# A windowed-attention kernel: the values projected together with queries and keys, in one group of 384 columns, and split at once into eight buffers

## The chip, the core and the metric

The kernel runs on one core of a Trainium2 chip (trn2). The core has TensorE (PE, with its weight loads PEld), VectorE (DVE), ScalarE (ACT), GpSimd (POOL) and SyncE (SP), each with its own stream of instructions; they wait for one another by semaphores. SBUF holds the data, PSUM (eight banks of 512 FP32 columns on each of 128 partitions) the results of TensorE. The metric is the device time of one execution in microseconds (us), lower is better.

## The reference, cut to what matters

A block of a Swin transformer (layer norm, attention in shifted windows of 8 x 8 with rotary embedding, a gated MLP), followed by self-attention over each image. The change touches only the first attention. x is (4, 32, 32, 128); there are 64 windows of 64 tokens, 16 heads of 8 channels.

```python
xs = jnp.roll(xn, (-SS[0], -SS[1]), axis=(1, 2))
xw = xs.reshape(B, nH, wh, nW, ww, DIM).transpose(0, 1, 3, 2, 4, 5).reshape(B_, N, DIM)
qkv = xw @ qkv_w.T + qkv_b
qkv = qkv.reshape(B_, N, 3, HEADS, HD).transpose(2, 0, 3, 1, 4)
q, k, v = (qkv[0], qkv[1], qkv[2])
q = _rope2d(q.reshape(-1, wh, ww, HD), tabs).reshape(B_, HEADS, N, HD)
k = _rope2d(k.reshape(-1, wh, ww, HD), tabs).reshape(B_, HEADS, N, HD)
attn = jnp.einsum('bhnd,bhmd->bhnm', q * scale, k)
attn = attn.reshape(B, nWin, HEADS, N, N) + attn_mask[None, :, None]
attn = jax.nn.softmax(attn.reshape(B_, HEADS, N, N), axis=-1)
out = jnp.einsum('bhnm,bhmd->bhnd', attn, v).transpose(0, 2, 1, 3).reshape(B_, N, DIM)
```

## The kernel before, in words

Two windows (128 tokens) make a pair; there are 32 pairs. The layer norm works in 8 chunks of 4 pairs. Precision is kept by splitting FP32 values into two FP16 parts, a high and a low one, so a product is three matmuls (high by high, high by low, low by high), and a projection has a fourth for the bias.

The attention stage is a software pipeline over steps n = -2 to 34, written as one `body(n, ...)` per engine; each engine does its own body in written order, so the order in the code is the order of the work. Steps -2 to 11 and 28 to 34 are unrolled, 12 to 27 are two rounds of a loop of eight steps. In step n:

- TensorE projects the queries and keys of pair n+2 (lines 866 and 868, `project`, into bank 4, 256 columns), turns the rows of pair n+1 (line 904), adds the mask and the scores of pair n (lines 876 and 885), in some steps turns a chunk of the layer norm (line 845), makes the turned scores of pair n-1 (876 and 897), multiplies probabilities by values for pair n-3 (line 956, 24 matmuls), projects the values of pair n-1 (866 and 868 again, 128 columns, into bank 6), and turns the queries of pair n with their maxima (line 904).
- VectorE multiplies queries and keys of pair n+2 by the two rope tables (line 1048, ta and tb), copies the turned rows of pair n+1 (line 1060, qk_t), makes the low part of the values of pair n-2 (line 1068, v_lo), takes the row maxima of pair n (line 1075), writes them in two parts into q_rows (lines 1080 and 1082), and normalises the result of pair n-3 (lines 1093 and 1097).
- ScalarE copies the rotated rows of pair n+2 (line 1117, q_rows and k_rows), takes the exponential for pair n-1 (line 1187), copies the turned queries (q_t), copies the high part of the values of pair n-1 (v_hi), and that of the probabilities (p_hi). `copy` is a helper, so all copies have line 1117; the tile tells them apart. In steps 3 to 10 it also normalises half a chunk (line 1131, xn) at the end of the step.
- GpSimd adds ta and tb into rot (line 1253), makes the low part of the probabilities of pair n-2 (line 1261, p_lo), and the low parts of the rows of pair n+2 (lines 1265 and 1267).
- SyncE copies keys from qk_t to k_t, four transfers a step (line 836).

The semaphores around the change: `qk_done` (projection of queries and keys done), `rope_done` (tb done, so bank 4 is free), `v_done` (values projected), `vhi_done`, `vlo_done` (their parts made), `mlo_done` (line 1082 done; the turning of the queries waits for it), `mask_hi` (mask copied to BF16). v_hi and v_lo have two buffers each. Each v buffer keeps zeros where the other window of the pair is, and a constant column; GpSimd writes both at the start (line 1222).

The mask copy of ScalarE stands in step -1, behind two transfers that it issues; TensorE waits for it ahead of step 0. The first steps of the MLP (`early`) are woven into steps 28 to 34.

## Time and profile before

| | us |
|---|---|
| median of 3 runs | 410.07 |
| lowest, highest | 408.0, 411.35 |
| profiled execution, its own time | 408.14 |
| its span in the trace | 406.3 |
| attention stage, first rope to last | about 12 to 190 |

| engine | busy us of the span |
|---|---|
| PE | 357.3 (88%) |
| DVE | 300.9 (74%) |
| ACT | 272.5 (67%) |
| POOL | 261.0 (64%) |

Busy time is the time in which at least one instruction of the engine ran. In a timeline each row has the start and the duration; "x3" merges three instructions of one kind that follow each other, and an instruction may start before the one ahead of it has written its last element. What stands in brackets is idle time of the engine before the row and what ended it.

### The profile page before, as it was taken

How to read it: one execution, taken by the hardware profiler on the slowest of the kernel's cores; microseconds unless marked ns; L12 is line 12 of the kernel's file. 1: busy time of each engine (PE TensorE's matmuls, PEld its weight loads, DVE VectorE, ACT ScalarE, POOL GpSimd, SP SyncE). 2: the span in 40 equal slices, each digit the busy share in tenths (PEclk: the TensorE clock that was granted, in tenths of full speed). 3: DMA queues.
4: the chain of work that ended last, by engine and by line, in shares of the span. 5: the costliest groups of instructions: out<-in, count | busy, mean ns of one | idle time of the engine just before them, and what ended most of it. 6: DMA issues, size and time to landing. Idle time of an engine off the chain costs nothing.

```text
span 406.3 us, 12124 instructions
## 1 busy us (share of the span) xinstructions
PE 357.3 (88%) x4700; PEld 223.4 (55%) x4700; DVE 300.9 (74%) x830; ACT 272.5 (67%) x436; POOL 261.0 (64%) x314
## 2 busy tenths in 40 slices
PE   2487999899998999998599999999989989989692
PEld 0244665555565666667355345553546757667472
DVE  6668888888888888887746767778657797884524
ACT  3467988887777787887635554444767867768480
POOL 7467967666767777797658665564235865868330
PEclk9999999999999999999989999999999999999787
DMA  5701110001101011110000100000101011010101
GB/s 173 250 15 27 29 27 26 25 24 30 31 27 29 25 29 29 29 29 3 0 3 2 26 2 0 2 2 0 28 0 28 2 52 27 2 54 2 53 2 55
DMA packets 15594, 12.19 MB, mean 30 GB/s; under 512 B 3991, under 2 KB 14136, under 8 KB 15544
## 3 DMA queue, kind: packets, MB, share of 16 engines
q1 hardware_dynamic: 14208, 10.96, 9.4%
q8 instruction: 34, 0.56, 0.6%
q10 hardware_dynamic: 1336, 0.54, 0.5%
q14 instruction: 16, 0.13, 0.1%
HBM read 4.15 MB, written 2.10 MB: 15 GB/s over the span
## 4 chain that ended last, share of the span: by engine, by line
PE 63%; DVE 15%; ACT 5%; DMA 5%; issue 5%; POOL 3%; SPq 2%; ACTq 1%; DVEq 0%; POOLq 0%
PE ps L347 8%; PE ps L1551 7%; PE ps L876 6%; PE ps L904 5%; PE ps L956 4%; PE ps L897 4%; DMA k_t<-qk_t 3%; PE ps L866 3%; PE ps L885 3%; PE ps L361 3%; SPq L836 2%; PE ps L868 2%; DVE ob L1687 2%; PE ps L1386 2%; DVE mx L1656 2%
## 5 line engine op out<-in xcount | busy, mean ns | idle before, releaser
L1738 POOL TENSOR_TENSOR el<-e,eh 128x1024 f16<-128x1024 f32 x28 | 59.7, 2131 | 42.0 <-ACT eh L1730 41.7
L1261 POOL TENSOR_TENSOR p_lo<-e_buf,p_hi 128x1024 f16<-128x1024 f32 x32 | 68.2, 2131 | 4.9 <-ACT p_hi L1117 2.9
L347 PE MATMUL ps<-y_t,fc_w 128*128 128x512 f16 x192 | 46.4, 383 | 4.0 <-POOL al L273 2.5
L1253 POOL TENSOR_TENSOR rot<-ta,tb 128x256 f32<-128x256 f32 x32 | 23.3, 728 | 38.9 <-DVE tb L1048 38.1
L1723 ACT ACTIVATE e<-ps 128x1024 f32<-128x1024 f32 x32 | 32.7, 1022 | 21.1 <-PE ps L1540 19.5
L1551 PE MATMUL ps<-val,eh 128*128 128x129 f16 x512 | 38.3, 225 | 7.5 <-DVE ob L1687 7.0
L876 PE MATMUL ps<-mask,identb 128*128 128x512 bf16 x128 | 39.4, 391 | 5.4 <-DMA k_t<-qk_t 5.2
L1075 DVE TENSOR_REDUCE ps<-ps 128x16 f32<-128x1024 f32 x32 | 39.4, 1233 | 6.0 <-PE ps L885 5.2
L1187 ACT ACTIVATE e_buf<-ps 128x1024 f32<-128x1024 f32 x32 | 32.7, 1023 | 14.5 <-PE ps L897 11.4
L1551 PEld LDWEIGHTS ps<-val,eh 128*128 128x128 f16 x512 | 32.8, 100 | 16.4 <-issue 9.9
L288 POOL TENSOR_TENSOR hl<-hid,hh 128x512 f16<-128x512 f32 x24 | 27.6, 1157 | 21.5 <-DVE yn L537 11.5
L1656 DVE TENSOR_REDUCE mx<-ps 128x1 f32<-128x1024 f32 x24 | 29.3, 1222 | 11.0 <-PE ps L1524 10.8
L1117 ACT ACTIVATE p_hi<-e_buf 128x1024 f16<-128x1024 f32 x32 | 33.8, 1057 | 0.8
L1730 ACT ACTIVATE eh<-e 128x1024 f16<-128x1024 f32 x32 | 33.7, 1054 | 0.7
L646 ACT ACTIVATE sg<-ps,fc_bias 128x512 f32<-128x512 f32 x32 | 21.9, 685 | 17.9 <-PE ps L347 17.6
L508 DVE SCALAR_TENSOR_TENSOR hid<-ps,fc_bias,sg 128x512 f32<-128x512 f32 x32 | 23.9, 746 | 11.2 <-PE ps L347 8.9
L866 PE MATMUL ps<-qkv_w,xn_all 128*128 128x128 f16 (+1 forms) x192 | 27.7, 255 | 5.0 <-ACT mask L1117 3.4
L904 PE MATMUL ps<-ident,q_rows 128*128 128x128 f16 x256 | 26.3, 227 | 6.0 <-DVE q_rows L1082 3.7
L347 PEld LDWEIGHTS ps<-y_t,fc_w 128*128 128x128 f16 x192 | 17.3, 98 | 25.9 <-issue 4.7
L1117 ACT ACTIVATE q_t<-ps 128x512 f16<-128x512 f16 x32 | 19.1, 596 | 10.7 <-PE ps L904 10.4
L897 PEld LDWEIGHTS ps<-q_t,k_t 128*64 128x64 f16 x1024 | 18.7, 113 | 13.6 <-issue 13.6
L1551 PE MATMUL ps<-val,el 128*128 128x129 f16 x256 | 23.8, 226 | 0.0
(166 smaller groups left out, 959.8 us busy)
## 6 DMA issues: line engine op xcount, KB each, us to landing
k_t<-qk_t SPq DMA_DIRECT2D x126, 32.0 KB, 1.9
x_all<-in_x SPq DMA_DIRECT2D x8, 256.0 KB, 4.9
out<-ob SPq DMA_DIRECT2D x8, 192.0 KB, 2.1
yr<-xr SPq DMA_DIRECT2D x16, 64.0 KB, 2.0
mask_f<-in_mask SPq DMA_DIRECT2D x1, 512.0 KB, 3.7
fc_w<-in_fc_w SPq DMA_DIRECT2D x1, 512.0 KB, 6.2
out<-ob SPq DMA_DIRECT2D x4, 128.0 KB, 2.4
fc_w<-in_fc_w SPq DMA_DIRECT2D x1, 256.0 KB, 6.1
```

What stands on the lines that cost most here:

```text
L347: last = pe.matmul(ps[:, bank, :], fc1_w16[:, ws, 128 * block_:128 * block_ + 128], y_t[:, v, ys, :], start=(n == 0), stop=(n == 2))
L866: pe.matmul(out, xn_all[:, at(i, 1), xs, :].rearrange("p a q -> p (a q)"), qkv_w16[:, ws, cols], start=(n == 0), stop=False, skip_group_ch ...
L876: pe.matmul(ps[:, bank + b, :].rearrange("p (h k) -> p h k", h=8), identb[:], mm, start=(part == 0), stop=False, skip_group_check=True)
L897: last = pe.matmul(ps[rows, ST_BANK + h // 8, WTOK * (h % 8):WTOK * (h % 8) + WTOK], keys[:, h % 4, h // 4, rows], queries[:, h // 4, rows ...
L904: last = pe.transpose(out[:, c, :], rows[:, 4 * c:4 * c + 4, :].rearrange("p h r -> p (h r)"), ident16[:])
L1075: dve.tensor_reduce(mx_ps, ps[:, S_BANK:S_BANK + 2, :].rearrange("p b (h k) -> p (b h) k", h=8), AX.X, ALU.max).then_inc(max_done, 1)
L1117: return act.activation(out, in_, ACT.Copy)
L1261: pool.tensor_tensor(p_lo[:, u], e_buf[:, u], p_hi[:, u], ALU.subtract).then_inc(plo_done, 1)
L1551: return pe.matmul(pv4[:, j, i, 0:DIM + 1], weights[:, T % H_BUFS, 128 * n:128 * n + 128], val[:, b % 2, part, m, 0:DIM + 1], start=first, ...
L1656: dve.tensor_reduce(mx[:, k:k + 1], two(S4), AX.X, ALU.max, negate=True).then_inc(max4_done, 1)
L1730: act.activation(eh[:, T % H_BUFS, :], e4[:, T % E_BUFS, :], ACT.Copy).then_inc(eh_done, 1)
L1738: pool.tensor_tensor(el[:, T % H_BUFS, :], e4[:, T % E_BUFS, :], eh[:, T % H_BUFS, :], ALU.subtract).then_inc(el_done, 1)
```

## The change

- The values are projected with queries and keys: each of the four matmuls of `project` has 384 columns instead of 256, into bank 4, for pair n+2. The group of four matmuls with 128 columns and its semaphore `v_done` are gone.
- v_hi and v_lo of pair n+2 are made in step n: v_hi at the front of ScalarE's step, behind `rope_done`; v_lo on VectorE at the place where v_lo of pair n-2 was, ahead of the maximum. The projection of the next pair waits for `vlo_done` too.
- v_hi and v_lo have eight buffers instead of two. GpSimd clears them as FP32 words (1152 on each partition for each, where it was 576 FP16 values).
- The mask is copied on ScalarE before step -2, and TensorE waits for it in step 0 ahead of the first scores, behind the projection of pair 2 and the turning of pair 1.
- The first turning of the MLP waits for `vlo_done` of all pairs instead of `rope_done`.

```diff
--- before.py
+++ after.py
@@ -118,8 +118,10 @@
         mask_f = until_mlp.enter_context(nc.sbuf_tensor("mask_f", [128, 2, WPAIRS, WTOK], F32))
         mask16 = until_mlp.enter_context(nc.sbuf_tensor("mask16", [128, 3, 2, WPAIRS, WTOK], BF16))
         xn_all = until_mlp.enter_context(nc.sbuf_tensor("xn_all", [128, PAIRS, 2, 128], F16))
-        v_hi = until_mlp.enter_context(nc.sbuf_tensor("v_hi", [128, 2, HP, 2, 2, HD + 1], F16))
-        v_lo = until_mlp.enter_context(nc.sbuf_tensor("v_lo", [128, 2, HP, 2, 2, HD + 1], F16))
+        v_hi_flat = until_mlp.enter_context(nc.sbuf_tensor("v_hi", [128, WPAIRS * HP * 4 * (HD + 1)], F16))
+        v_hi = v_hi_flat[:].rearrange("p (n h e r d) -> p n h e r d", n=WPAIRS, h=HP, e=2, r=2)
+        v_lo_flat = until_mlp.enter_context(nc.sbuf_tensor("v_lo", [128, WPAIRS * HP * 4 * (HD + 1)], F16))
+        v_lo = v_lo_flat[:].rearrange("p (n h e r d) -> p n h e r d", n=WPAIRS, h=HP, e=2, r=2)
 
         q_rows = until_mlp.enter_context(nc.sbuf_tensor("q_rows", [128, BUFS, HEADS, ROWS], F16))
         k_rows = until_mlp.enter_context(nc.sbuf_tensor("k_rows", [128, 2, HEADS, ROWS], F16))
@@ -172,7 +174,6 @@
         ln_ready = sem("ln_ready")
 
         qk_done = sem("qk_done")
-        v_done = sem("v_done")
         rope_done = sem("rope_done")
         vhi_done = sem("vhi_done")
         vlo_done = sem("vlo_done")
@@ -464,7 +465,7 @@
             def early(left):
                 if left == 5:
 
-                    pe.wait_ge(rope_done, PAIRS)
+                    pe.wait_ge(vlo_done, PAIRS)
                     turn_a_waits(0)
                     turn_a(0, 0)
                 if left == 4:
@@ -767,7 +768,7 @@
             S_BANK, ST_BANK, QKV_BANK, T1_BANK, T2_BANK, PV_BANK = 0, 2, 4, 5, 6, 7
             qkv_ps = ps[:, QKV_BANK, :]
             mx_ps = ps[:, S_BANK, 0:HEADS]
-            v_ps = ps[:, T2_BANK, 256:256 + DIM]
+            v_ps = ps[:, QKV_BANK, 2 * DIM:3 * DIM]
             t1_ps = ps[:, T1_BANK, :].bitcast(F16).rearrange("p (a c q) -> p a c q", a=2, c=4)
             t2_ps = ps[:, T2_BANK, 0:256].bitcast(F16).rearrange("p (c q) -> p c q", c=4)
             pv_ps = ps[:, PV_BANK, 0:HP * 4 * (HD + 1)].rearrange("p (h e r d) -> p h e r d", h=HP, e=2, r=2)
@@ -914,7 +915,8 @@
                         wait(pe, rope_done, n + 2)
 
                         pe.wait_ge(ln_ready, (n + 2) // TPC + 1 if isinstance(n, int) and n < LOOP_FROM else CHUNKS)
-                        project(qkv_ps[:, 0:2 * DIM], n + 2, slice(0, 2 * DIM)).then_inc(qk_done, 1)
+                        wait(pe, vlo_done, n + 2)
+                        project(qkv_ps[:, 0:3 * DIM], n + 2, slice(0, 3 * DIM)).then_inc(qk_done, 1)
                     if at_step(n, -2):
 
                         pe.wait_ge(mask_top, 1)
@@ -933,6 +935,8 @@
                         turn(t1_ps[:, 1], k_rows[:, v]).then_inc(t1_done, 1)
                     if valid(n, 0):
 
+                        if at_step(n, 0):
+                            pe.wait_ge(mask_lo if parts > 1 else mask_hi, 1)
                         pe.wait_ge(kz_ready[u], it * 64 + 64)
                         wait(pe, mlo_done, n)
                         scores(qk_t[:, u, 0], k_t[:, r], w, parts).then_inc(s_done, 1)
@@ -954,14 +958,9 @@
                             out = pv_ps[:, hp].rearrange("p e r d -> p (e r d)")
                             for k, (p, vals) in enumerate(((p_hi, v_hi), (p_hi, v_lo), (p_lo, v_hi))):
                                 last = pe.matmul(out, p[:, v, 2 * hp:2 * hp + 2, :].rearrange("p h q -> p (h q)"),
-                                                 vals[:, v, hp].rearrange("p e r d -> p (e r d)"),
+                                                 vals[:, (w - 3) % WPAIRS, hp].rearrange("p e r d -> p (e r d)"),
                                                  start=(k == 0 and hp == 0), stop=(k == 2), skip_group_check=True)
                         last.then_inc(pv_done, 1)
-                    if valid(n, 1):
-
-                        wait(pe, vlo_done, n - 1)
-                        wait(pe, q2_ready, n)
-                        project(v_ps, n - 1, slice(2 * DIM, 3 * DIM)).then_inc(v_done, 1)
                     if valid(n, 0):
                         wait(pe, mlo_done, n + 1)
                         wait(pe, q2_ready, n)
@@ -973,7 +972,6 @@
                 first_steps(lambda n, it, r: body(n, it, r, 1))
 
                 def other_pairs(parts):
-                    pe.wait_ge(mask_lo if parts > 1 else mask_hi, 1)
                     other_steps(pe, lambda n, it, r: body(n, it, r, parts), mlp_pe(pe)[1])
 
                 return rest[0], other_pairs
@@ -1060,14 +1058,15 @@
                         dve.tensor_copy(qk_t[:, v], t1_ps).then_inc(qt_ready, 1)
                     if at_step(n, -1):
                         ln_stats_of(3)
-                    if valid(n, 2):
-
-                        dve.wait_ge(vhi_done, n - 1)
+                    if valid(n, -2):
+
+                        dve.wait_ge(vhi_done, n + 3)
                         for e in range(2):
                             rows = slice(64 * e, 64 * e + 64)
                             last = dve.tensor_tensor(
-                                v_lo[rows, u, :, e, :, 0:HD], v_ps[rows, :].rearrange("p (h r d) -> p h r d", r=2, d=HD),
-                                v_hi[rows, u, :, e, :, 0:HD], ALU.subtract)
+                                v_lo[rows, (w + 2) % WPAIRS, :, e, :, 0:HD],
+                                v_ps[rows, :].rearrange("p (h r d) -> p h r d", r=2, d=HD),
+                                v_hi[rows, (w + 2) % WPAIRS, :, e, :, 0:HD], ALU.subtract)
                         last.then_inc(vlo_done, 1)
                     if valid(n, 0):
 
@@ -1145,6 +1144,8 @@
                 copy(qkv_w16[:, 0, :], w_scaled[:, 0:3 * DIM]).then_inc(qkv_w_hi, 1)
                 ln_hi_of(0)
                 ln_norm_of(1)
+                act.wait_ge(mask_loaded, 16)
+                copy(mask16[:, 0], mask_f[:]).then_inc(mask_hi, 1)
 
                 def body(n, it, w):
                     r = w % BUFS
@@ -1154,6 +1155,13 @@
                         mlp_act(act)[2](LAST - n)
                     if valid(n, -2):
 
+                        act.wait_ge(rope_done, n + 3)
+                        wait(act, pv_done, n - 5)
+                        for e in range(2):
+                            rows = slice(64 * e, 64 * e + 64)
+                            last = copy(v_hi[rows, (w + 2) % WPAIRS, :, e, :, 0:HD],
+                                        v_ps[rows, :].rearrange("p (h r d) -> p h r d", r=2, d=HD))
+                        last.then_inc(vhi_done, 1)
                         act.wait_ge(r_done, n + 3)
                         copy(q_rows[:, (r + 2) % BUFS, :, 0:16].rearrange("p h (r d) -> p h r d", r=2),
                              rot[:, u, 0].unsqueeze(2).broadcast_to([128, HEADS, 2, HD]))
@@ -1168,8 +1176,6 @@
                         for j in (2, 3):
                             rows = slice(ROWS * j, ROWS * j + ROWS)
                             act.dma_start(k_t[rows, 0, j], qk_t[rows, 0, 1]).then_inc(kz_ready[0], 16)
-                        act.wait_ge(mask_loaded, 16)
-                        copy(mask16[:, 0], mask_f[:]).then_inc(mask_hi, 1)
                         ln_norm_of(2)
                     if at_step(n, 0):
                         ln_norm_of(3)
@@ -1192,13 +1198,7 @@
                         copy(q_t2[:, u], t2_ps).then_inc(q2_ready, 1)
                     if valid(n, 1):
 
-                        act.wait_ge(v_done, n)
                         wait(act, pv_done, n - 2)
-                        for e in range(2):
-                            rows = slice(64 * e, 64 * e + 64)
-                            last = copy(v_hi[rows, v, :, e, :, 0:HD],
-                                        v_ps[rows, :].rearrange("p (h r d) -> p h r d", r=2, d=HD))
-                        last.then_inc(vhi_done, 1)
                         act.wait_ge(exp_done, n)
                         copy(p_hi[:, v], e_buf[:, v]).then_inc(phi_done, 1)
                     if at_step(n, 0):
@@ -1214,7 +1214,7 @@
             def _(pool):
 
 
-                for k, (part, value) in enumerate(((v_hi[:], 0.0), (v_lo[:], 0.0),
+                for k, (part, value) in enumerate(((v_hi_flat[:].bitcast(F32), 0.0), (v_lo_flat[:].bitcast(F32), 0.0),
                                                    (v_hi[0:64, :, :, 0, :, HD:HD + 1], WSCALE),
                                                    (v_hi[64:128, :, :, 1, :, HD:HD + 1], WSCALE))):
                     if k >= 1:
```

How it stands on ScalarE, in a step between 5 and 10 that ends with half a normalisation. q_rows and k_rows are the rotated rows, e_buf the exponential, q_t the turned queries, xn the normalised chunk. Before, from the exponential on:

```order
L1187 ACTIVATE e_buf<-ps 128x1024
L1117 ACTIVATE q_t<-ps 128x512
L1117 ACTIVATE v_hi<-ps 64x8x2x8 x2
L1117 ACTIVATE p_hi<-e_buf 128x1024
L1131 ACTIVATE xn<-x_all,nmr,rstd 128x128 x2
L1117 ACTIVATE q_rows<-rot 128x16x16
L1117 ACTIVATE k_rows<-rot 128x32x8
```

And of the change (its line numbers differ by a few):

```order
L1193 ACTIVATE e_buf<-ps 128x1024
L1116 ACTIVATE q_t<-ps 128x512
L1116 ACTIVATE p_hi<-e_buf 128x1024
L1130 ACTIVATE xn<-x_all,nmr,rstd 128x128 x2
L1116 ACTIVATE v_hi<-ps 64x8x2x8 x2
L1116 ACTIVATE q_rows<-rot 128x16x16
L1116 ACTIVATE k_rows<-rot 128x32x8
```

v_hi stood between q_t and p_hi; it now stands behind p_hi and xn, ahead of the next q_rows.

On TensorE, where one step goes over to the next, from the last product with the values on. Before:

```order
L956 MATMUL ps<-v_hi,p_lo 128x36
L866 MATMUL ps<-qkv_w,xn_all 128x128 x3
L868 MATMUL ps<-qkv_b,sel 128x128
L904 MATMUL ps<-ident,q_rows 128x128 x4
L866 MATMUL ps<-qkv_w,xn_all 128x256 x3
L868 MATMUL ps<-qkv_b,sel 128x256
L904 MATMUL ps<-ident,q_rows 128x128 x4
L904 MATMUL ps<-ident,k_rows 128x128 x4
```

And now:

```order
L960 MATMUL ps<-v_hi,p_lo 128x36
L905 MATMUL ps<-ident,q_rows 128x128 x4
L867 MATMUL ps<-qkv_w,xn_all 128x384 x3
L869 MATMUL ps<-qkv_b,sel 128x384
L905 MATMUL ps<-ident,q_rows 128x128 x4
L905 MATMUL ps<-ident,k_rows 128x128 x4
```

The four matmuls of 128 columns ahead of the turning of q_rows are gone, and the projection behind it has 384 columns. VectorE's instructions keep their order; only the pair that v_lo works on is another.

## Rows read from the trace of the kernel before

**Rows 1.** Windows view: busy us of PE, PEld, DVE, ACT, POOL; clock, DMA, GB/s
```profile
140.00:150.00 10.00, 10.00 (x185) 6.39 (x184) 8.94 (x24) 8.23 (x15) 7.88 (x11) 1.00 0.10 26
```

**Rows 2.** Timeline, VectorE, one step: start us, duration us, instruction, [idle before]
```profile
147.32 0.23 DVE L1082 SCALAR_TENSOR_TENSOR q_rows<-ps,q_rows 128x16 f16<-128x16 f32 x1
...
148.66 0.42 DVE L1048 TENSOR_TENSOR ta<-ps,rope 128x256 f32<-128x256 f32 x1 [0.26 <-PE ps L868]
149.00 0.42 DVE L1048 TENSOR_TENSOR tb<-ps,rope 128x256 f32<-128x256 f32 x1
149.33 0.68 DVE L1060 COPY qk_t<-ps 128x1024 f16<-128x1024 f16 x1
149.93 0.59 DVE L1068 TENSOR_TENSOR v_lo<-ps,v_hi 64x128 f16<-64x128 f32 x2
150.54 1.23 DVE L1075 TENSOR_REDUCE ps<-ps 128x16 f32<-128x1024 f32 x1
...
152.07 0.23 DVE L1082 SCALAR_TENSOR_TENSOR q_rows<-ps,q_rows 128x16 f16<-128x16 f32 x1
```

**Rows 3.** Timeline, TensorE, the same step
```profile
147.15 0.33 PE L866 MATMUL ps<-qkv_w,xn_all 128*128 128x128 f16 x3
147.41 0.23 PE L868 MATMUL ps<-qkv_b,sel 33*128 33x128 f16 x1
147.60 0.40 PE L904 MATMUL ps<-ident,q_rows 128*128 128x128 f16 x4
147.91 0.50 PE L866 MATMUL ps<-qkv_w,xn_all 128*128 128x256 f16 x3
148.34 0.28 PE L868 MATMUL ps<-qkv_b,sel 33*128 33x256 f16 x1
```

**Rows 4.** Timeline, ScalarE, the same step
```profile
148.04 0.60 ACT L1117 ACTIVATE q_t<-ps 128x512 f16<-128x512 f16 x1 [0.37 <-PE ps L904]
148.53 0.59 ACT L1117 ACTIVATE v_hi<-ps 64x128 f16<-64x128 f32 x2
149.14 1.06 ACT L1117 ACTIVATE p_hi<-e_buf 128x1024 f16<-128x1024 f32 x1
```

**Rows 5.** Timeline, ScalarE, a step with half a normalisation
```profile
60.68 1.06 ACT L1117 ACTIVATE p_hi<-e_buf 128x1024 f16<-128x1024 f32 x1
61.64 0.86 ACT L1131 ACTIVATE xn<-x_all,nmr,rstd 128x128 f32<-128x128 f32 x2
62.41 0.40 ACT L1117 ACTIVATE q_rows<-rot 128x256 f16<-128x256 f32 x1
```

**Rows 6.** Timeline, VectorE, line 1082 in steps 3, 11 and 29
```profile
42.81 0.23 DVE L1082 SCALAR_TENSOR_TENSOR q_rows<-ps,q_rows 128x16 f16<-128x16 f32 x1
...
85.57 0.23 DVE L1082 SCALAR_TENSOR_TENSOR q_rows<-ps,q_rows 128x16 f16<-128x16 f32 x1
...
175.85 0.23 DVE L1082 SCALAR_TENSOR_TENSOR q_rows<-ps,q_rows 128x16 f16<-128x16 f32 x1
```

**Rows 7.** Timelines of VectorE and TensorE at the start
```profile
12.42 0.42 DVE L1048 TENSOR_TENSOR ta<-ps,rope 128x256 f32<-128x256 f32 x1 [0.68 <-PE ps L868]
...
13.27 0.85 PE L866 MATMUL ps<-qkv_w,xn_all 128*128 128x256 f16 x3
...
14.48 0.42 DVE L1048 TENSOR_TENSOR ta<-ps,rope 128x256 f32<-128x256 f32 x1 [1.25 <-PE ps L868]
...
18.59 0.38 DVE L996 BATCH_NORM_AGGREGATE mv<-stats 128x2 f32<-128x6 f32 x4
...
20.22 0.82 PE L866 MATMUL ps<-qkv_w,xn_all 128*128 128x256 f16 x3 [3.38 <-ACT mask L1117]
```

**Rows 8.** Timelines of VectorE and ScalarE at the end of the attention stage
```profile
184.13 0.57 DVE L1068 TENSOR_TENSOR v_lo<-ps,v_hi 64x128 f16<-64x128 f32 x2
...
190.83 0.60 ACT L1117 ACTIVATE v_hi<-ps 64x128 f16<-64x128 f32 x2
```

**Rows 9.** Waits of TensorE, 86 to 176 us: in total, times, longest us
```profile
PE ps L876 <- DMA k_t<-qk_t: 2.7, 3, 0.9
```

## The prediction

> **What bounds the kernel now.** I began with the busy time of each engine in ten microseconds of the attention stage [rows 1]. TensorE is busy for all ten of ten microseconds there, VectorE for 8.94, ScalarE for 8.23, and the chain of waits of the page runs through TensorE alone in this stretch. That invites the reading that TensorE is the bound and that every matmul taken from it is time won. The rows of VectorE and TensorE in order of time say more [rows 2, 3]. Step n is one pass of the body. In it VectorE multiplies by the rope tables (ta, tb), copies the turned rows (qk_t), makes v_lo, takes the row maximum and writes it in two parts (the second, line 1082, I call the end of the maximum). From ta at 148.66 to the end of the maximum at 152.30 (152.07 and 0.23) it is never idle. Its one idle time in a step is 0.26 us before ta, and the matmul of line 868 ends it. On TensorE the turning of q_rows (line 904) starts at 147.60, which is 0.05 us after the maximum ended at 147.55, and the projection of queries and keys follows it at once. So there is a ring: end of the maximum, 0.05 us, turning q_rows 0.31, projection 0.75 until ta, 3.64 us of VectorE in a row, end of the next maximum: 4.75 us, exactly the distance of the two rows of line 1082 [rows 2]. TensorE's own work fills the same 4.75 us, so both bind at once. Removing work from TensorE opens only one of two locks.
>
> **The change part by part, in a step from the 12th on.** On TensorE the four matmuls for the values go. From their start to the turning behind them are 0.45 us [rows 3]. In return each of the four matmuls of the projection has 128 columns more. Three of 128 columns take 0.26 us up to the fourth, three of 256 take 0.43, so 128 columns cost 0.17/3 = 0.057 us and the four cost 0.23. TensorE gains 0.22 us a step. But the 0.45 us stood beside the ring, between the multiplication by the probabilities and a turning that waits for the maximum anyway, whereas the 0.23 us stand inside the ring: ta waits for the last matmul of the group. That alone makes a step 4.98 us.
>
> The second term is v_hi. Its copy on ScalarE was made behind q_t and ahead of p_hi, and VectorE took v_lo a step later, with the copy done 0.8 us before (149.12 against 149.93) [rows 2, 4]. Now v_lo of pair n+2 follows in the same step as its rope, and ahead of the maximum. v_hi waits for the rope because all three parts share one bank. Count from the turning of q_rows as zero. ta starts at 0.31 + 0.75 + 0.23 = 1.29, tb ends 0.76 later at 2.05. ScalarE has taken q_t at 0.44 and p_hi at 0.93, and is free at about 1.90, so v_hi starts at 2.10 by the rope, ends at 2.69, and v_lo starts at 2.74. By VectorE's own order it would start at 1.29 + 1.27 = 2.56. VectorE thus stands still for 0.18 us. From v_lo to the maximum are 0.61 us, to line 1082 1.53, its length 0.23, to the turning 0.05: a ring of 5.16 us [rows 2, 3]. Behind the standing v_lo is queued the maximum, and for that waits TensorE. Before, 18 steps lay between 85.57 and 175.85 [rows 6]: 90.28 us, of which 3 late key transfers take part [rows 9]. After, 18 x 5.16 = 92.9: **+2.6 us**. The late transfers (0.9 us of waiting each) cost nothing then, since the keys get 0.41 us more per step before the scores want them and the scores wait for nobody for some 0.5 us. The bound from below is no stall for v_hi: 18 x 4.98 = 89.6, -0.6. From above each stall as in the next paragraph: 18 x 5.72, +12.7.
>
> The Trainium skill, page "PSUM — Partial Sum Buffer", section "PSUM bank collisions raise a hardware error", says that two engines may not be in one bank and quarter of the partitions at once, even both reading. By this rule v_hi can't be laid beside the rope in the shared bank; here the program's waits keep them apart and no row before shows a clash.
>
> **Steps 4 to 11.** In steps 3 to 10 ScalarE has half a normalisation (xn, two of line 1131) behind p_hi [rows 5]. The v_hi of the next step is now queued behind both, and VectorE and the maximum behind v_hi. This makes a longer ring: v_hi 0.59 and 0.05; v_lo to the maximum 0.61; to line 1082 and through it 1.76; 0.05; turning to q_t 0.44; q_t 0.49; p_hi to xn 0.96; xn 0.77 [rows 2 to 5]. That is 5.72 us. Before, the 8 steps from 42.81 to 85.57 took 42.76 us [rows 6]; after, 8 x 5.72 = 45.8: **+3.0 us**. The halves themselves come 0.6 us sooner than before, since v_hi is no longer ahead of p_hi, so the waits of TensorE for xn shrink; that is no gain in this ring. Bounds: 5.16 a step gives -1.5; on top of 5.72, 0.7 us in the four odd steps for the copy of xn_all on VectorE, +5.8.
>
> **The start.** TensorE's columns cost twice as much here: three matmuls of 256 and the last one take 1.21 us from 13.27 to ta at 14.48, against 0.75 [rows 7]. 128 more on four cost then 4 x 0.11 = 0.43. The rope of pair 0 comes at 12.85 instead of 12.42, ends at 13.6, v_hi and v_lo take 1.3, and the projection of pair 1, which now waits for v_lo, starts at 14.9 instead of 13.27. Its ta is at 14.9 + 1.21 + 0.43 = 16.55 instead of 14.48. Behind it VectorE worked without a gap until 18.97 (4.49 us, with the statistics of two chunks) [rows 7], and v_lo of pair 1 is behind all that: 16.55 + 4.49 + 0.65 = 21.7. Projection of pair 2 waits for it: 21.75 instead of 20.22, and takes 0.43 longer. So the first maximum is about **+1.9 us**. What is won there, the mask copy (1.06 us, now at about 12 beside idle ScalarE) that ended TensorE's wait of 3.38 us, is covered by the new wait. Where that cover is wrong, the start gains up to 1.5. The larger clearing of v_hi and v_lo on GpSimd ends before the statistics that it waits for, within some tenths. Steps 1 to 3 take 0.4 longer each, as the ring: **+1.2**.
>
> **The end.** From step 30 on no pair enters, so v_lo of pair 29 no longer precedes the maximum of pair 31 (0.60), and v_hi of pair 31 (0.60) no longer precedes p_hi [rows 8]; TensorE's last values group saves 0.1. Both are in the chain of waits: **-1.3**. What follows is not touched.
>
> Sum: 1.9 + 1.2 + 3.0 + 2.6 - 1.3 = +7.4. On the profiled execution (408.14) that is 415.5; on the median of the three runs (410.07) 417.5. Part of what separates the runs should be late transfers, which a longer ring hides, so I take the middle, **416.5**.
>
> **Rivals.**
> A. TensorE alone is the bound, and the 0.05 us after the maximum is chance. Then 30 steps x 0.22 = 6.6 us and the end's 1.3 are won: 400 to 402. For it: [rows 1] and the page's chain. Against: the same 0.05 us after line 1082 in most steps, and ta's idle time ended by the projection. Chance 0.08. By the Trainium skill, "TensorE: Matmul & The Clock Gate", section "Wait — 56ns, not 53.3ns?", a warm matmul costs its columns at 2.4 GHz and 2.5 ns; then four of 128 are worth 0.22 us, as much as the columns added, and the rival would give some 408. The 0.45 us of [rows 3] disagrees, as the place before a turning costs more than columns.
> B. The steps get slower as I say but less so: the start gains 1 instead of losing 1.9 because the mask no longer holds TensorE, or ScalarE's halves come soon enough, so that steps 4 to 11 stay as they were. Each takes about 3 us off: 410 to 413. Chance 0.19.
> C. More is lost: the stall of v_hi is doubled by what waits behind it (q_rows, k_rows, then GpSimd's parts, then the turning a step later). GpSimd has 1 us to spare in a step; it decides where v_hi ends over 0.8 us later than the rope needs. At 5.5 us a step for 18 steps: +6 on top, 421 to 428. Chance 0.10.
> The forecast itself, 413 to 421: 0.63.
>
> **Numbers.** The middle 416.5. Leaving out A and the further half of B and C at their ends gives 410 to 422. One per cent is 4.1 us, about what a measurement of this kernel tells from no change. Faster by over 1% (under 406): A, 0.08. Within 1% (406 to 414.2): B and the low end of the forecast, 0.22. Slower: 0.70.
>
> **What would show it.** In the profile after: TensorE below 9.3 of 10 us in the middle of the stage, with gaps before the turning of q_rows that the maximum ends; VectorE idle before v_lo, ended by v_hi, 0.2 us a step late and over 1 us in steps 4 to 11; line 1082's counterpart every 5.16 us; first maximum at about 26, not 24.2. The prediction is wrong if v_lo never waits, if steps are 4.75 or shorter, or if the first projection of pair 2 comes before 20.2. TensorE's granted clock is 1.00 in [rows 1]; if it falls in the new gaps, the columns cost double and the time lies above the range.

## The result: 2.5% slower, and the profile after

| | before | after |
|---|---|---|
| median of 4 runs each, us | 409.04 | 418.75 |
| lowest, highest | 408.0, 411.35 | 415.8, 421.92 |
| profiled execution, its own time | 408.14 | 415.8 |
| its span | 406.3 | 414.0 |

The ratio is 1.0245, with a 95% interval of 1.0191 to 1.0299: slower, by 1.9 to 3.0%. The forecast was 416.5, its range 410 to 422, the chance of slower 0.70. The median before was 410.07 when the prediction was made, and a fourth run brought it to 409.04.

The windows view of the kernel after, the ten microseconds of [rows 1] (busy us of PE, PEld, DVE, ACT, POOL; clock, DMA, GB/s):

```profile
140.00:150.00 10.00, 9.06 (x168) 5.41 (x165) 8.37 (x21) 7.75 (x14) 6.93 (x10) 1.00 0.09 23
```

TensorE fell from 10.00 to 9.06, and so did every other engine: less work is done in the same time, by a ring that is in no one engine. One step of it on VectorE, against [rows 2]:

```profile
146.27 0.42 DVE L1046 TENSOR_TENSOR ta<-ps,rope 128x256 f32<-128x256 f32 x1 [0.47 <-PE ps L869]
146.62 0.41 DVE L1046 TENSOR_TENSOR tb<-ps,rope 128x256 f32<-128x256 f32 x1
146.95 0.68 DVE L1058 COPY qk_t<-ps 128x1024 f16<-128x1024 f16 x1
147.78 0.60 DVE L1066 TENSOR_TENSOR v_lo<-ps,v_hi 64x128 f16<-64x128 f32 x2 [0.15 <-ACT v_hi L1116]
...
149.94 0.23 DVE L1081 SCALAR_TENSOR_TENSOR q_rows<-ps,q_rows 128x16 f16<-128x16 f32 x1
```

On TensorE, against [rows 3]:

```profile
145.00 0.40 PE L905 MATMUL ps<-ident,q_rows 128*128 128x128 f16 x4 [0.58 <-DVE q_rows L1081]
145.31 0.66 PE L867 MATMUL ps<-qkv_w,xn_all 128*128 128x384 f16 x3
145.90 0.33 PE L869 MATMUL ps<-qkv_b,sel 33*128 33x384 f16 x1
```

On ScalarE, against [rows 4]:

```profile
145.44 0.60 ACT L1116 ACTIVATE q_t<-ps 128x512 f16<-128x512 f16 x1 [0.56 <-PE ps L905]
145.93 1.05 ACT L1116 ACTIVATE p_hi<-e_buf 128x1024 f16<-128x1024 f32 x1
147.14 0.60 ACT L1116 ACTIVATE v_hi<-ps 64x128 f16<-64x128 f32 x2 [0.16 <-DVE tb L1046]
```

And in a step with half a normalisation, against [rows 5]:

```profile
58.72 1.05 ACT L1116 ACTIVATE p_hi<-e_buf 128x1024 f16<-128x1024 f32 x1
59.67 0.87 ACT L1130 ACTIVATE xn<-x_all,nmr,rstd 128x128 f32<-128x128 f32 x2
60.44 0.59 ACT L1116 ACTIVATE v_hi<-ps 64x128 f16<-64x128 f32 x2
```

The turning at 145.00 now waits 0.58 us for the maximum, where before it came without a gap. ta comes 1.27 us behind it (forecast 1.29), v_hi starts at 2.14 (2.10) by the rope, v_lo at 2.78 (2.74) by v_hi. The step shown is one of 5.22 us; in those of 5.14 v_hi follows the rope by 0.03 us instead of 0.11, and v_lo starts 1.42 us behind ta, where it was 1.27 before. So v_hi costs 0.15 us in such a step (forecast 0.18), of which 0.07 is idle time. The view of the waits leaves out what is under 0.15 us. The waits of VectorE, first from 46 to 92 us (steps 4 to 11), then from 92 to 186 (12 to 29): in total, times, longest us.

```profile
DVE v_lo L1066 <- ACT v_hi L1116: 5.3, 8, 0.7
DVE ta L1046 <- PE ps L869: 2.0, 4, 0.5
```

```profile
DVE ta L1046 <- PE ps L869: 8.7, 18, 1.0
DVE v_lo L1066 <- ACT v_hi L1116: 0.7, 3, 0.3
```

TensorE in that second stretch, against [rows 9]:

```profile
PE ps L905 <- DVE q_rows L1081: 8.9, 16, 0.8
PE ps L877 <- DMA k_t<-qk_t: 0.7, 2, 0.4
```

VectorE's line 1081, the counterpart of 1082 in [rows 6], in steps 3, 11 and 29:

```profile
46.09 0.23 DVE L1081 SCALAR_TENSOR_TENSOR q_rows<-ps,q_rows 128x16 f16<-128x16 f32 x1
...
91.75 0.23 DVE L1081 SCALAR_TENSOR_TENSOR q_rows<-ps,q_rows 128x16 f16<-128x16 f32 x1
...
186.13 0.23 DVE L1081 SCALAR_TENSOR_TENSOR q_rows<-ps,q_rows 128x16 f16<-128x16 f32 x1
```

VectorE and then TensorE at the start, against [rows 7]:

```profile
13.79 0.42 DVE L1046 TENSOR_TENSOR ta<-ps,rope 128x256 f32<-128x256 f32 x1 [1.21 <-PE ps L869]
...
15.21 0.60 DVE L1066 TENSOR_TENSOR v_lo<-ps,v_hi 64x128 f16<-64x128 f32 x2 [0.61 <-ACT v_hi L1116]
...
21.77 0.57 DVE L1066 TENSOR_TENSOR v_lo<-ps,v_hi 64x128 f16<-64x128 f32 x2
```

```profile
15.95 1.12 PE L867 MATMUL ps<-qkv_w,xn_all 128*128 128x384 f16 x3 [1.10 <-DVE v_lo L1066]
...
22.48 1.12 PE L867 MATMUL ps<-qkv_w,xn_all 128*128 128x384 f16 x3 [4.01 <-DVE v_lo L1066]
```

The wait of 3.38 us for the mask has become one of 4.01 us for v_lo. From these, and the same rows at the other steps, the two profiled executions differ by 7.7 us of span:

| stretch | before | after | difference | forecast |
|---|---|---|---|---|
| to the first maximum | 24.23 | 26.89 | +2.7 | +1.9 |
| to the end of the maximum of step 3 | 18.8 | 19.4 | +0.6 | +1.2 |
| steps 4 to 11 | 42.8 | 45.7 | +2.9 | +3.0 |
| steps 12 to 29 | 90.3 | 94.4 | +4.1 | +2.6 |
| steps 30, 31 | 10.4 | 9.2 | -1.2 | -1.3 |
| the rest (MLP, second attention) | 219.8 | 218.4 | -1.4 | 0 |

### The profile page after: what moved, and what is told of

It is laid out like the page before. It is cut to its first block, busy times and chain, and to the rows that moved or that the text cites. A ratio compares the mean times of both kernels' runs of the same rounds, so it can differ in the third digit from the quotient of the medians.

```text
span 414.0 us, 11850 instructions
## 1 busy us (share of the span) xinstructions
PE 352.8 (85%) x4572; PEld 216.1 (52%) x4572; DVE 305.4 (74%) x830; ACT 272.8 (66%) x436; POOL 261.8 (63%) x314
## 4 chain that ended last, share of the span: by engine, by line
PE 42%; DVE 29%; ACT 11%; issue 8%; POOL 6%; DMA 1%; SPq 1%; DVEq 0%; ACTq 0%; POOLq 0%
PE ps L348 8%; DVE ps L1074 7%; PE ps L1551 7%; DVE v_lo L1066 4%; ACT v_hi L1116 3%; PE ps L362 3%; PE ps L905 3%; PE ps L867 3%; ACT p_hi L1116 3%; DVE ob L1687 2%; DVE mx L1656 2%; PE ps L1386 2%; ACT xn L1130 2%; PE ps L1534 2%; DVE ta L1046 2%
## 5 line engine op out<-in xcount | busy, mean ns | idle before, releaser
L1193 ACT ACTIVATE e_buf<-ps 128x1024 f32<-128x1024 f32 x32 | 32.8, 1024 | 14.3 <-PE ps L898 14.2
L1656 DVE TENSOR_REDUCE mx<-ps 128x1 f32<-128x1024 f32 x24 | 29.3, 1222 | 10.5 <-PE ps L1524 10.2
L905 PEld LDWEIGHTS ps<-ident,q_rows 128*128 128x128 f16 x256 | 14.7, 99 | 27.4 <-DVE q_rows L1081 21.1
L867 PE MATMUL ps<-qkv_w,xn_all 128*128 128x384 f16 x96 | 22.4, 344 | 7.5 <-DVE v_lo L1066 5.1
```

The lines of the kernel that those rows point to most:

```text
L867: pe.matmul(out, xn_all[:, at(i, 1), xs, :].rearrange("p a q -> p (a q)"), qkv_w16[:, ws, cols], start=(n == 0), stop=False, skip_group_ch ...
L905: last = pe.transpose(out[:, c, :], rows[:, 4 * c:4 * c + 4, :].rearrange("p h r -> p (h r)"), ident16[:])
L1193: act.activation(e_buf[:, v], ps[:, ST_BANK:ST_BANK + 2, :].rearrange("p b (h q) -> p (b h) q", h=8), ACT.Exp).then_inc(exp_done, 1)
L1656: dve.tensor_reduce(mx[:, k:k + 1], two(S4), AX.X, ALU.max, negate=True).then_inc(max4_done, 1)
```

## The experiments

Below, "end 29" is the end of the maximum of step 29 in the profiled execution (before 176.08, after 186.36), and a ratio is to the kernel before, run on the same chip (its medians there were 408.1, 408.8 and 408.4), with a 95% interval. The kernel after was not run again on these chips. The intervals of v_lo behind, narrow, the halves sooner and the start all overlap the one of after (1.0191 to 1.0299), and that of everything at once reaches into it, so a difference of 1 to 4 us between two of these medians proves little. What these runs show is read from the lengths of the steps, in one profiled execution each.

**The mask alone.** The kernel before with the one part of the change that promised a gain. TensorE's wait for the mask moves too:

```diff
+                        if at_step(n, 0):
+                            pe.wait_ge(mask_lo if parts > 1 else mask_hi, 1)
...
-                    pe.wait_ge(mask_lo if parts > 1 else mask_hi, 1)
...
                 ln_norm_of(1)
+                act.wait_ge(mask_loaded, 16)
+                copy(mask16[:, 0], mask_f[:]).then_inc(mask_hi, 1)
...
-                        act.wait_ge(mask_loaded, 16)
-                        copy(mask16[:, 0], mask_f[:]).then_inc(mask_hi, 1)
                         ln_norm_of(2)
```

> The kernel before with one part of the change only: the mask is copied on ScalarE ahead of step -2, and TensorE waits for it ahead of the first scores. Theory (the start is set by the values' parts, not by the mask): with the values left as before, the projection of pair 2 starts about 18 instead of 20.22 and the first maximum (24.23 before) comes 1 to 1.8 us sooner, limited then by the transfers of the keys; total 1 to 2 us less, 407 to 408. Rival (the move of the mask itself costs, by its 1.06 us ahead of the rows of pair 0): first maximum up to 1 us later. The steps behind stay at 4.75 us.

Measured 409.25 us, ratio 1.0023 (0.9994 to 1.0051). The first maximum came at 23.65, 0.6 us sooner, less than the 1 to 1.8 expected: TensorE now waits 2.17 us ahead of the first scores, for the transfers of the keys. End 29 was 0.9 sooner, and nothing of it is left in the time.

**v_lo behind the maximum.** The kernel after, with v_lo out of the ring that I had named:

```diff
-                    if valid(n, -2):
-
-                        dve.wait_ge(vhi_done, n + 3)
...
-                        last.then_inc(vlo_done, 1)
...
                                                  op0=ALU.mult, op1=ALU.subtract).then_inc(mlo_done, 1)
+                    if valid(n, -2):
+
+                        dve.wait_ge(vhi_done, n + 3)
...
+                        last.then_inc(vlo_done, 1)
```

> The changed kernel with v_lo moved on VectorE from ahead of the maximum to behind its second part (behind the write that the turning of the queries waits for). Theory (v_lo, and v_hi ahead of it, stand inside the ring from maximum to maximum): both leave the ring, and VectorE no longer waits for ScalarE's v_hi. Steps 12 to 29: about 4.7 us each instead of 5.14, steps 4 to 11 about 4.9 instead of 5.71. The projection now waits for v_lo, some 0.3 us of idle TensorE a step. In all 12 to 15 us less than the changed kernel, 402 to 406, so below the kernel before. Rival (the wider projection or TensorE's own work sets the step): steps stay at 5.0 or above, total above 412.

Measured 416.71, ratio 1.0172 (1.0098 to 1.0246). The time that I expected was missed. VectorE and then TensorE of this kernel in a late step:

```profile
149.88 1.23 DVE L1064 TENSOR_REDUCE ps<-ps 128x16 f32<-128x1024 f32 x1 [0.19 <-PE ps L886]
...
151.41 0.23 DVE L1071 SCALAR_TENSOR_TENSOR q_rows<-ps,q_rows 128x16 f16<-128x16 f32 x1
151.50 0.59 DVE L1078 TENSOR_TENSOR v_lo<-ps,v_hi 64x128 f16<-64x128 f32 x2
...
154.85 1.23 DVE L1064 TENSOR_REDUCE ps<-ps 128x16 f32<-128x1024 f32 x1 [0.19 <-PE ps L886]
```

```profile
151.70 0.40 PE L905 MATMUL ps<-ident,q_rows 128*128 128x128 f16 x4
152.34 0.66 PE L867 MATMUL ps<-qkv_w,xn_all 128*128 128x384 f16 x3 [0.25 <-DVE v_lo L1078]
```

v_hi stops nobody any more, and the steps fell from 5.14 to 4.97 us (154.85 - 149.88). But the bank is held until v_lo is made, so the projection waits for v_lo, the scores come behind the projection, and the maximum behind the scores: a second ring of 4.97. End 29 came at 182.03, 4.3 us sooner than after; the median is only 2.0 lower. In the profiled execution step 31 took 7.84 us, with this row of TensorE in it:

```profile
190.59 1.03 PE L877 MATMUL ps<-mask,identb 128*128 128x512 bf16 x2 [2.88 <-DMA k_t<-qk_t]
```

The 1.03 us of two matmuls, 0.59 in other steps, show the clock at its lower level there.

**A narrow projection.** The kernel after, with three of the four matmuls 256 columns wide (the low parts and the bias of the values are left out):

```diff
                                   qkv_w16[:, ws, cols], start=(n == 0), stop=False, skip_group_check=True)
+                        out, cols = qkv_ps[:, 0:2 * DIM], slice(0, 2 * DIM)
```

> The changed kernel, but only the first of the four matmuls of the projection has 384 columns, the other three 256: of the values the low parts and the bias are left out. It takes 3 x 0.057 = 0.17 us out of the wait of ta and out of TensorE's work, and changes no wait. Theory of two rings: steps 12 to 29, whose ring holds the projection, go from 5.14 to 4.97 us; steps 4 to 11, whose ring runs through ScalarE (v_hi, v_lo, maximum, q_t, p_hi, xn) and not through the projection, stay at 5.71. Total 3 to 4 us less than the changed kernel. Rival (one bound for all, TensorE): both go down by 0.17 us, 5 us in all. Rival (columns cost nothing, only the stall does): neither moves.

Measured 416.35, ratio 1.0184 (1.0138 to 1.0231). Line 1082 in two steps in a row:

```profile
158.95 0.23 DVE L1082 SCALAR_TENSOR_TENSOR q_rows<-ps,q_rows 128x16 f16<-128x16 f32 x1
...
163.93 0.23 DVE L1082 SCALAR_TENSOR_TENSOR q_rows<-ps,q_rows 128x16 f16<-128x16 f32 x1
```

Most late steps that took 5.14 us fell to 4.97 to 5.00, by three times 0.057 us; steps 5 to 11 stayed at 5.71. End 29 came 1.8 us sooner (184.52), and the median is 2.4 lower where 3 to 4 were expected. So the columns are in the late ring and not in the early one: the early one runs through ScalarE, and the rope has slack there.

**The halves of the normalisation sooner.** The kernel after, xn moved from behind p_hi to behind the rows:

```diff
+                    for ahead in (1, 2):
+                        c = ln_chunk(n, -ahead)
+                        if c and c > 3:
+                            ln_norm_of(c, range(2 * (2 - ahead), 2 * (2 - ahead) + 2))
                     if ln_chunk(n):
...
-                    for ahead in (1, 2):
-                        c = ln_chunk(n, -ahead)
```

> The changed kernel with ScalarE's half normalisations of steps 3 to 10 moved inside their step, from behind p_hi to behind k_rows, ahead of the exponential. Theory: they leave the ring of steps 4 to 11, which falls to that of the later steps, 5.15 to 5.4 us instead of 5.71 (a little above, as the exponential is now later than q_t in the odd steps); steps 12 to 29 stay at 5.14. Total 2.5 to 4.5 us less than the changed kernel. Rival (steps 4 to 11 are longer for TensorE's turning of the chunk, or for VectorE's statistics and copy of it): they stay at 5.6 to 5.7.

Measured 416.71, ratio 1.0192 (1.0145 to 1.0238). Steps 4 to 11 took 42.3 us instead of 45.7, and VectorE's waits from 46 to 92 us are these:

```profile
DVE ta L1046 <- PE ps L869: 2.3, 5, 0.5
DVE ps L1074 <- PE ps L886: 1.3, 3, 0.7
```

The wait for v_hi (5.3 us, 8 times) is gone, so the third term has the cause that the prediction gave it. Of the 3.4 us won here 2.0 are left at end 29 (184.32), and in the median: steps 1 to 3 took 18.6 us instead of 17.7, with TensorE's granted clock at half from 42.4 to 45.8 us.

**The start.** The kernel after, with GpSimd's clearing of v_hi and v_lo moved behind its first statistics, and v_lo of pair 1 ahead of the statistics of chunk 3 (the waits for the clearing move with it, and ScalarE's first instruction reads another tile):

```diff
-                for k, (part, value) in enumerate(((v_hi_flat[:].bitcast(F32), 0.0), (v_lo_flat[:].bitcast(F32), 0.0),
...
                 pool.memset(k_t[:, 0:2].bitcast(F32), 0.0).then_inc(keys_set, 1)
...
+                for k, (part, value) in enumerate(((v_hi_flat[:].bitcast(F32), 0.0), (v_lo_flat[:].bitcast(F32), 0.0),
...
-                    if at_step(n, -1):
-                        ln_stats_of(3)
                     if valid(n, -2):
...
                         last.then_inc(vlo_done, 1)
+                    if at_step(n, -1):
+                        ln_stats_of(3)
```

> The changed kernel with two edits of the start. (a) GpSimd fills the v buffers behind the statistics of the first two chunks instead of ahead of all. The fill ahead took 3.5 us where it took 1.8 before, and the first normalisation came 0.97 us later (7.98 against 7.01); it should be back at about 7.0 and the first projection at 11.2 instead of 12.13. (b) v_lo of pair 1 stands ahead of the statistics of chunk 3 on VectorE, 1.28 us sooner, so the projection of pair 2 comes at about 20.3 instead of 22.48 and the first maximum at 24.7 instead of 26.89. Steps as in the changed kernel (5.71 and 5.14). Total 2 us less, if nothing later takes it back. Rival (the mask or the keys' transfers set the first scores): first maximum at 26 or later.

Measured 420.0, ratio 1.0274 (1.0225 to 1.0323), where 2 us less than after was expected. The first maximum came at 25.66 instead of 26.89, all by v_lo: the first rope stayed at 13.78, though the statistics that it comes from were back in their old place. VectorE, and GpSimd beside it:

```profile
8.67 2.01 DVE L1024 TENSOR_SCALAR qkv_b<-b_sum 33x384 f16<-33x384 f32 x1
```

```profile
8.56 0.91 POOL L1235 TENSOR_TENSOR qkv_w<-w_scaled,qkv_w 128x384 f16<-128x384 f32 x1
9.41 1.06 POOL L1243 MEMSET v_hi<- 128x1152 f32 x1
```

The small instruction of line 1024 ran for 2.01 us, beside the weights' low part and the whole first clearing, and ended 0.2 us behind the latter (10.68, 10.47); in the kernel before it took 0.37. In the kernel after it took 1.08 and ended at 10.68 too, 0.2 us behind the weights' low part (10.47). That GpSimd held it up is read from the times alone, but it would explain why the first rope did not move: what was won ahead of this instruction was lost in it. By step 3 the 1.2 us were lost again (end of its maximum at 47.06, after 46.32), in steps in which TensorE's granted clock stood at half (28.8 to 32.2 and 42.4 to 45.8 us; after only 30.4 to 33.8).

**Fewer value matmuls.** The kernel before, with two of the four matmuls for the values left out, and with them the low parts of the product, to ask whether TensorE's work alone bounds it:

```diff
-                    for n, (xs, ws) in enumerate(((0, 0), (0, 1), (1, 0))):
+                    for n, (xs, ws) in enumerate(((0, 0), (0, 1), (1, 0))[:3 if cols.start == 0 else 1]):
```

> The kernel before, with two of the four matmuls left out of each projection of the values (the products with the low parts). TensorE has 0.17 us less to do per step, at a place that is not in the ring from maximum to turning to projection to rope to maximum. Theory of the ring: steps 21 to 29 stay at 4.75 us and a gap opens on TensorE ahead of the turning; in steps 4 to 11, where TensorE comes late to the turning behind a chunk's turning, some 0.1 us each may be won; total 0 to 1.5 us less. Rival A of the prediction (TensorE alone is the bound): 4.58 us a step, 5 us less in all.

Measured 407.76, ratio 0.9985 (0.9951 to 1.0019). Line 1082 in two steps in a row:

```profile
148.02 0.23 DVE L1082 SCALAR_TENSOR_TENSOR q_rows<-ps,q_rows 128x16 f16<-128x16 f32 x1
...
152.78 0.23 DVE L1082 SCALAR_TENSOR_TENSOR q_rows<-ps,q_rows 128x16 f16<-128x16 f32 x1
```

4.76 us, as before, with less on TensorE. What was taken from it is 0.11 us a step: the group of four takes 0.42 us up to the next turning where TensorE comes late to it, the group of two 0.31. In most late steps TensorE now stands idle for 0.08 to 0.12 us ahead of the turning. Rival A falls: by it some 3 us would have been won (0.11 in 30 steps), and the interval allows 2 at most.

**Everything at once.** The kernel after with v_lo behind the maximum from step 0 on and the edits of the start; first(n) is true below step 0, and v_lo stands under both new lines:

```diff
+                    if first(n):
+                        if valid(n, -2):
...
                     if at_step(n, -1):
                         ln_stats_of(3)
...
+                    if not first(n):
+                        if valid(n, -2):
```

> The changed kernel with v_lo behind the second part of the maximum from step 0 on, v_lo of pairs 0 and 1 as early as in the start experiment, and the v buffers filled behind the first statistics. If the rings and the start are what the theories say, the savings add: steps at 4.7 us (4.9 in steps 4 to 11), first maximum at 24.7: 400 to 404 us, below the kernel before. If one saving only uncovers another bound (VectorE is busy some 4.5 us a step), the total is at 405 to 408.

Measured 415.08, ratio 1.0163 (1.0122 to 1.0204); 400 to 408 was expected and missed. Steps of 4.97 again; end 29 at 180.92, still 4.8 us later than in the kernel before. With the values in the bank of the rope, neither order that was tried pays. Making the values as early as here in a bank of their own was not tried.

**The larger buffers alone.** The kernel before with eight buffers and their clearing, of which the steps use two as before:

```diff
-        v_hi = until_mlp.enter_context(nc.sbuf_tensor("v_hi", [128, 2, HP, 2, 2, HD + 1], F16))
+        v_hi_flat = until_mlp.enter_context(nc.sbuf_tensor("v_hi", [128, WPAIRS * HP * 4 * (HD + 1)], F16))
...
-                for k, (part, value) in enumerate(((v_hi[:], 0.0), (v_lo[:], 0.0),
+                for k, (part, value) in enumerate(((v_hi_flat[:].bitcast(F32), 0.0), (v_lo_flat[:].bitcast(F32), 0.0),
```

> The kernel before, with nothing changed but the size of the two value buffers (eight pairs instead of two, cleared by GpSimd as FP32 words); the steps still use the first two. It isolates a term that I took as nothing. Theory: the larger clearing delays all that is behind it on GpSimd and on ScalarE by 0.9 to 1.0 us, so the first rope stands at 13.3 to 13.4 instead of 12.42, the first maximum 0.6 to 1.0 later than 24.23; steps stay at 4.75 us; the whole 0.3 to 1.2 us above before. Rival: the clearing is done before it matters, the first rope stays at 12.4 and the late start of the change comes from the order of ScalarE's work (mask copy ahead of the first steps): then the time is that of before within 0.3.

Measured 409.74, ratio 1.001 (0.9981 to 1.0039). GpSimd at the start of this kernel, then of the kernel before:

```profile
0.74 1.06 POOL L1224 MEMSET v_hi<- 128x1152 f32 x1 [0.29 <-POOLq L1838]
1.85 1.06 POOL L1224 MEMSET v_lo<- 128x1152 f32 x1
2.97 1.33 POOL L1224 MEMSET v_hi<- 64x128 f16 x2
4.36 1.81 POOL L1226 MEMSET k_t<- 128x2048 f32 x1
6.21 0.20 POOL L1232 TENSOR_TENSOR veps<-mv,ln_const 128x4 f32<-128x4 f32 x1
```

```profile
2.58 1.81 POOL L1224 MEMSET k_t<- 128x2048 f32 x1
5.24 0.20 POOL L1230 TENSOR_TENSOR veps<-mv,ln_const 128x4 f32<-128x4 f32 x1 [0.85 <-DVE mv L996]
```

Before, GpSimd stood 0.85 us idle ahead of the statistics; the clearing takes 1.78 us more (k_t starts at 4.36, not 2.58), and 0.97 of it are left over. The first rope comes at 13.36 instead of 12.42, the first maximum at 25.09 instead of 24.23.

**A version below both.** In the trace of before, the turning of q_rows lags 0.6 to 1.5 us behind the maximum in the odd steps from 3 to 11, longest in steps 7 and 11, in which TensorE waits for xn. The edit that brought xn behind the rows, made to the kernel before:

```diff
+                    for ahead in (1, 2):
+                        c = ln_chunk(n, -ahead)
...
                     if ln_chunk(n):
...
-                    for ahead in (1, 2):
-                        c = ln_chunk(n, -ahead)
```

> The kernel before, with the two halves of a normalisation that ScalarE makes in steps 3 to 10 moved from the end of the step (behind p_hi) to behind q_rows and k_rows of the same step, ahead of the exponential. Theory: in the trace of before the turning of q_rows lags 0.6 to 1.5 us behind the end of the maximum in the odd steps among 4 to 11, since TensorE waits for the normalised chunk; 5.2 us of such lag in all. With the halves half a step sooner most of it goes: steps 4 to 11 fall from 5.35 us in the mean to 4.9 to 5.1, end of the maximum of step 11 at 82.5 to 84 instead of 85.80, the whole 2 to 4 us below before (404 to 407). Rival: ScalarE now holds up the exponential by 0.77 us, and the product with the values and all that is behind it on TensorE with it: the steps stay at 5.3 or get longer, and the time stays or rises by 1 to 3 us.

Measured 407.23, ratio 0.9963 (0.9936 to 0.9989): faster by 0.4%, less than the 2 to 4 us expected. TensorE's waits from 42 to 88 us, before and then in this kernel:

```profile
PE ps L845 <- ACT xn L1131: 1.8, 2, 0.9
PE ps L876 <- DMA k_t<-qk_t: 1.3, 2, 1.1
```

```profile
PE ps L876 <- DMA k_t<-qk_t: 1.9, 4, 0.6
```

The wait for xn is gone, the lags of steps 7 and 11 fell from 1.51 to 0.57 us and those of steps 3, 5 and 9 stayed. 1.3 us are won by step 11, 2.8 by step 29.

## Why the prediction was right, and where it was not

**Two locks.** The ring is shown. Less work on TensorE moves nothing (fewer value matmuls); fewer columns in the ring give back just their duration (narrow projection); with the wait for v_hi gone the ring is shorter (v_lo behind). That TensorE's own work would have held the steps at 4.75 us with a shorter ring, the second lock, no run asked.

**Steps 12 to 29, forecast 5.16 us each.** The ring was right: 13 of the 18 steps took 5.13 to 5.22. The term was too small, 4.1 against 2.6, since I took all 18 alike. The 90.3 us before hold 4.8 above 18 times 4.75, and I let all of that vanish. The waits for late keys went from 2.7 us to 0.7, but 1.9 us above 18 times 5.14 stayed, 1.15 of them in two steps. In step 12 the projection waits for the copy of the last normalised chunk. TensorE:

```profile
92.73 0.66 PE L867 MATMUL ps<-qkv_w,xn_all 128*128 128x384 f16 x3 [0.30 <-DVE xn_all L1009]
...
134.79 0.66 PE L867 MATMUL ps<-qkv_w,xn_all 128*128 128x384 f16 x3 [0.31 <-issue]
```

The second row is step 20, where the loop of eight steps goes round. Both gaps lie in the ring, between the turning and the projection. They make up some 0.6 of the 1.15 us; what the rest is was not followed. Before, steps 12 and 20 stood out too (6.24 and 5.86 us), which I could have read and did not.

**Steps 4 to 11, forecast 5.72.** All eight took 5.70 or 5.71, and moving xn ended them. One sign was stated wrongly: VectorE was to stand idle for over 1 us before v_lo in these steps, and it did so for 0.59 to 0.73. The sum did not use that figure; 5.72 less 4.98 gives 0.74.

**The start, forecast +1.9.** The chain was right (projection of pair 2 at 22.48 behind v_lo of pair 1), its entry was not: "within some tenths" for the clearing is the step that failed. It costs 0.94 us at the first rope, and that is shown alone. The 128 columns more on four matmuls cost 0.38 us there (15.95 to ta at 17.54, against 1.21 before), forecast 0.43. The mask gives 0.6 where the keys are next in the way, and nothing where v_lo is. Steps 1 to 3 lost 0.6 and not 1.2: they took 5.9, 6.4 and 4.7 us before, and only the third, which was as short as the ring, lost what I had forecast (0.37; the others 0.08 and 0.17).

**The end, forecast -1.3.** -1.2. That "what follows is not touched" is wrong by -1.4 in this pair of executions. From the end of step 29 on, the profiled executions of all eleven kernels took 227.4 to 234.1 us (before 230.2, after 227.6), a spread as large as most terms here; the stretches of lower clock fall at other places in each. The stretch from the maximum of step 31 to the end goes with how long the clock was at half in it: low for 14.6 and 15.0 us in the shortest two (the start 218.1, after 218.4), for 18.2 before (219.8) and for 29.2 in the longest (everything at once, 223.2). Over the eleven traces the two go together with a correlation of 0.90. So the -1.4 may be one stretch of 3.4 us fewer. What sets their places was not tried.

**The sum.** +7.4 forecast, +7.7 measured in the profiled pair, but by errors that cancel (+0.8, -0.6, +1.5, -1.4). The agreement of the two sums is luck. The median of after lies 3 us above its profiled execution, which was the fastest of the four; that of before 0.9 above. The medians differ by 9.7 us, and the 2 us beyond the profiled pair are in no trace. The four runs of after were 415.8, 418.18, 421.92 and 419.33 us at a mean granted clock of 0.978, 0.970, 0.957 and 0.973: the slowest has the lowest clock. But of the kernel before, a run of 408.83 us had 0.965 and one of 411.18 had 0.977, so the clock alone does not settle it. I took the middle because a longer ring would hide late transfers and so narrow the runs; they spread over 6 us after and over 3 before.

**The rivals.** A fell. B and C did not come: the start did not gain, and v_hi never came 0.8 us later than the rope wants it. C's time (421) was reached by one run, the one of the lowest clock; its mechanism was not seen.

## What to carry to other kernels

Before work is taken from the engine that looks full, find the ring: follow one step backwards until it meets itself, and ask of each moved instruction whether it enters. Here 0.42 to 0.45 us beside the ring were traded for 0.23 in it, and a result that shared a bank with the rope pulled two engines' copies in. In this program a bank is free when the last of its parts is read, so parts with different readers are better kept in different banks, as the kernel before has them; no run tried the wider projection that way.

## What the runs showed of the hardware that was not expected

Some of VectorE's FP32 instructions from SBUF to SBUF stood still beside a long instruction of GpSimd. In the kernel after, at the first turning of the MLP, VectorE and GpSimd:

```profile
196.48 4.04 DVE L538 TENSOR_SCALAR yn<-x,rstd,nmr 128x128 f32<-128x128 f32 x4
```

```profile
195.71 4.21 POOL L1261 TENSOR_TENSOR p_lo<-e_buf,p_hi 128x1024 f16<-128x1024 f32 x2
```

The four take 4.04 us where they took 1.68 before; one of them alone takes from 0.34 to 2.16 us, and 2.16 is the length of one p_lo (2.13). This fits what the Trainium skill says on the page "SBUF — State Buffer", section "SBUF: two separate sides": VectorE in a two-port mode and GpSimd exclude each other for a whole instruction. That these four run in such a mode the trace does not show. Each v_lo and maximum, which read PSUM, kept their durations (0.60 and 1.23). A clearing does it as well: in the kernel after, the scaling of the gains (line 1015, four columns) took 1.19 us instead of 0.14 and ended at 6.20, as GpSimd's clearing of k_t ended at 6.17. It is no rule for all: line 1002, of the same kind and shape as the four above, kept 0.33 to 0.36 us beside GpSimd's instructions on four columns, one of which lasted 1.01 us.

TensorE's granted clock fell to half, its lower level of 1.2 GHz, for 3.4 to 13.7 us at a time, at other places in nearly every kernel. With v_lo behind it fell at 189.6, inside the wait of 2.88 us; in the kernel after at 197.6, where TensorE had been busy for 9.27 of the ten microseconds before. The two kernels that had saved 4.3 and 5.4 us by step 29 (v_lo behind, everything at once) had it at half for 10 to 14 us between 189 and 204, and their medians are 2.0 and 3.7 us lower than that of after. But saving time is not what brings it: with fewer value matmuls (from 189.2) and with the larger buffers alone (from 188.7), which had saved nothing by step 29, it was at half for 10.2 and 13.7 us there too. What it follows is open.
